# Expert down bias from one stacked pass of score and table rows, scores turned later and copied by the scalar engine

## What is computed

```python
logits = x @ router_weight.T + router_bias
top_val, top_idx = jax.lax.top_k(logits, 4)
router_scores = zeros.at[rows, top_idx].set(softmax(top_val))      # (T, E)
gate_up = einsum('th,ehd->etd', x, gate_up_proj) + gate_up_proj_bias[:, None, :]
glu = gate * sigmoid(gate * 1.702)                                 # gate, up: clipped halves
out = einsum('etd,edh->eth', (up + 1.0) * glu, down_proj) + down_proj_bias[:, None, :]
out = (out * router_scores.T[:, :, None]).sum(axis=0)
```

## Time and profile before

| | us |
|---|---|
| three runs: median (lowest to highest) | 222.13 (221.68 to 222.31) |
| the profiled execution, its own time | 221.69 |
| its span (first to last instruction) | 219.6 |
| busy in the span: PE / PEld / DVE | 212.3 / 176.9 / 159.5 |
| busy in the span: ACT / POOL | 129.7 / 84.2 |

### The profile page before, as it was taken

The page is one execution under the profiler, slowest core; times in us unless marked ns, Lnnn a source line. Parts: engine busy times, 40 slices in busy tenths (PEclk is TensorE's granted clock), DMA queues, the critical chain, the costliest instruction groups (busy, mean ns, idle before and its releaser), DMA issues.

```text
span 219.6 us, 4392 instructions
## 1 busy us (share of the span) xinstructions
PE 212.3 (97%) x1394; PEld 176.9 (81%) x1394; DVE 159.5 (73%) x438; ACT 129.7 (59%) x248; POOL 84.2 (38%) x70
## 2 busy tenths in 40 slices
PE   7999999998999999999999999999999999999995
PEld 2688766776776789788898898898898898898893
DVE  3579897879468558898895785785786786786754
ACT  2238789859632714656765665675676666666340
POOL 6259989201002010246535615615516516416000
PEclk9999999999999999999999999999999999999999
DMA  6994420000000000031442142142241241310002
GB/s 181 328 383 152 145 100 0 0 4 0 3 0 0 3 0 1 0 87 61 145 143 87 60 143 72 72 143 54 89 143 40 103 143 28 115 48 0 0 0 96
DMA packets 7997, 17.41 MB, mean 79 GB/s; under 512 B 928, under 2 KB 3120, under 8 KB 7856
## 3 DMA queue, kind: packets, MB, share of 16 engines
q1 hardware_dynamic: 7552, 16.94, 23.7%
q10 hardware_dynamic: 432, 0.31, 0.5%
HBM read 16.72 MB, written 0.52 MB: 79 GB/s over the span
## 4 chain that ended last, share of the span: by engine, by line
PE 88%; DVE 5%; ACT 3%; issue 3%; POOL 1%; DVEq 0%; ACTq 0%; POOLq 0%
PE PS L1160 37%; PE PS L1176 20%; PE PS L932 3%; PE PS L1044 3%; PE PS L1029 3%; PE PS L984 3%; PE PS L920 2%; PE PS L1127 2%; ACT pr L438 2%; PE PS L1017 2%; PE PS L946 2%; PE PS L970 2%; PE PS L1205 2%; PE PS L997 2%; PE PS L974 1%
## 5 line engine op out<-in xcount | busy, mean ns | idle before, releaser
L308 POOL TENSOR_TENSOR WLg<-raw_g,WHg 128x1024 fp32r<-128x1024 f32 x16 | 38.3, 2396 | 70.8 <-ACT WHg L408 70.6
L1160 PE MATMUL PS<-XH,WHg 128*128 128x512 f32 x120 | 47.0, 391 | 0.0
L1160 PE MATMUL PS<-XL,WHg 128*128 128x512 f32 x120 | 46.9, 391 | 0.0
L1160 PE MATMUL PS<-XH,WLg 128*128 128x512 f32 x120 | 46.7, 389 | 0.0
L840 DVE TENSOR_SCALAR pt<-pt 128x512 f32<-128x512 f32 x30 | 25.0, 833 | 22.4 <-ACT pt L532 22.4
L1176 PE MATMUL PS<-WHd,HH 128*128 128x256 f32 x120 | 34.0, 283 | 0.0
L1176 PE MATMUL PS<-WLd,HH 128*128 128x256 f32 x120 | 34.0, 283 | 0.0
L1176 PE MATMUL PS<-WHd,HL 128*128 128x256 f32 x120 | 34.0, 283 | 0.0
L532 ACT ACTIVATE pt<-PS,bup 128x512 f32<-128x512 f32 x30 | 20.7, 688 | 15.2 <-PE PS L1160 15.2
L538 ACT ACTIVATE HH<-pt 128x512 fp32r<-128x512 f32 x30 | 18.9, 629 | 16.1 <-DVE pt L844 15.7
L438 ACT ACTIVATE pr<-masked,nmax 128x128 f32<-128x128 f32 x64 | 23.7, 444 | 5.9 <-DVE nmax L718 5.9
(11 more groups left out here) (162 smaller groups left out, 355.8 us busy)
## 6 DMA issues: line engine op xcount, KB each, us to landing
raw_g<-we_d SPq DMA_DIRECT2D x16, 512.0 KB, 4.0
raw_w<-we_d SPq DMA_DIRECT2D x16, 256.0 KB, 2.7
ctxT<-ctxT_d SPq DMA_DIRECT2D x1, 1024.0 KB, 10.4
ctx_sb<-ctx_d SPq DMA_DIRECT2D x1, 1024.0 KB, 12.5
wqkv<-wqkv_d SPq DMA_DIRECT2D x3, 256.0 KB, 4.9
out_d<-x SPq DMA_DIRECT2D x4, 128.0 KB, 1.8
rows<-rows_d SPq DMA_DIRECT2D x1, 264.0 KB, 6.3
x<-x_d ACTq DMA_DIRECT2D x2, 128.0 KB, 3.0
```

The source lines that it names most:

```text
L308: g.tensor_tensor(WLg[slot][:, :, :, :].rearrange("p k g f -> p (k g f)"), raw_g[slot][:, :], WHg[slot][:, :, :, :].rearrange("p k g f -> ...
L1160: i = t.matmul(PS[:, 2 * m + part, :], w[slot][:, k, part, m * P:(m + 1) * P], xx[:, k, :], start=(n == 0), stop=(n == 3 * KD - 1))
```

## The change

The table of biases is written three times into a stack of 80 rows (blocks at rows 0, 32 and 64, zero between). The first two blocks hold its high part, the third its low part. The scores are laid out in the same 80 columns: high, low, high. One float32r product over the 80 rows then gives high x high + low x high + high x low.

- SP fetches the table three times, after POOL has zeroed the stack.
- POOL zeroes `dbias`, `low_rows` and `score3`, and makes `dbias3` from the table with three operations: round to `dbias_high`, multiply by `low_rows` (0 in the first 64 rows, -1 in the last 16), add to the table. These stand behind the first `rstds`.
- DVE adds three operations after the score: copy rounded to the high block, subtract for the low block, copy of the high block.
- PE transposes 80 columns instead of 16, after the gate part of the second half of gate_up(1) and no longer between the halves, into bank 6. `weighted_biases` works on `dbias3`.
- The copy to `scoreT` moves from DVE to ACT, behind the two `high` operations of expert 0.

```diff
+            sp.wait_ge(dbias_zero, 1)
+            for block in range(3):
+                sp.dma_start(dbias[block * 32:block * 32 + E, :], dbias_d).then_inc(dbias_in, 16)
...
+            g.memset(dbias[:, :], 0.0).then_inc(dbias_zero, 1)
+            link(g.memset(low_rows[:, :], -1.0))
+            link(g.memset(low_rows[0:64, :], 0.0))
+            g.memset(score3[:, :, :], 0.0).then_inc(score3_zero, 1)
...
-            for n in range(1, 5):
-                rstds(n)
+            rstds(1)
+            pool.wait_ge(dbias_in, 48)
+            g.tensor_copy(dbias_high[:, :], dbias[:, :]).then_inc(dbias_split, 1)
+            pool.wait_ge(dbias_split, 1)
+            g.tensor_scalar(dbias_high[:, :], dbias_high[:, :].bitcast(F32), low_rows[:, 0:1], None, ALU.mult).then_inc(dbias_split, 1)
+            pool.wait_ge(dbias_split, 2)
+            g.tensor_tensor(dbias3[:, :], dbias[:, :], dbias_high[:, :].bitcast(F32), ALU.add).then_inc(dbias_split, 1)
+            rstds(2)
...
                 high(1)
+                if isinstance(e, int) and e == 0:
+                    act.wait_ge(scoreT_ps, 1)
+                    a.activation(scoreT[:, :], PS[0:ROWS3, 6, :], ACT.Copy).then_inc(scoreT_done, 1)
...
-            v_.tensor_tensor(score[:, :, :], esel[:, :, :], erec[:, :].unsqueeze(2).to_broadcast([P, NC, E]), ALU.mult
-                             ).then_inc(score_done, 1)
+            link(v_.tensor_tensor(score[:, :, :], esel[:, :, :], erec[:, :].unsqueeze(2).to_broadcast([P, NC, E]), ALU.mult))
+            dve.wait_ge(score3_zero, 1)
+            high, low_, again = (score3[:, :, n * 32:n * 32 + E] for n in range(3))
+            link(v_.tensor_copy(high.bitcast(F32R), score[:, :, :]))
+            v_.tensor_tensor(low_, score[:, :, :], high, ALU.subtract)
+            v_.tensor_copy(again, high).then_inc(score_done, 1)
...
                 if isinstance(e, int) and e == 0:
-                    dve.wait_ge(scoreT_ps, 1)
-                    v_.tensor_copy(scoreT[:, :], PS[0:E, 5, :]).then_inc(scoreT_done, 1)
                     low(1)
...
-                    i = t.transpose(PS[0:E, 5, c * P:(c + 1) * P], score[:, c, :], ident[:, :])
+                    i = t.transpose(PS[0:ROWS3, 6, c * P:(c + 1) * P], score3[:, c, :], ident[:, :])
...
-                    if m == 0 and isinstance(e, int) and e == 1:
-                        turn_scores()
+                        if m == 1 and part == 0 and isinstance(e, int) and e == 1:
+                            turn_scores()
...
-                pe.wait_ge(dbias_in, 16)
+                pe.wait_ge(dbias_split, 3)
-                    t.matmul(PS[:, 6 + c // 2, (c % 2) * D:(c % 2 + 1) * D], scoreT[:, c * P:(c + 1) * P], dbias[:, :], start=True, stop=True
+                    t.matmul(PS[:, 6 + c // 2, (c % 2) * D:(c % 2 + 1) * D], scoreT[:, c * P:(c + 1) * P], dbias3[:, :], start=True, stop=True
```

More of the change, by code:

```diff
@@ L37 @@
 DW = D * KD
+ROWS3 = 2 * 32 + E
 def decoder_layer(nc, x_d, ctx_d, ctxT_d, wqkv_d, wo_d, params_d, rows_d, mask_d, dbias_d, we_d, out_d):
@@ L69, in decoder_layer @@
         mask8 = sb("mask8", [P, B * M], U8)
-        dbias = sb("dbias", [E, D])
+        dbias = sb("dbias", [ROWS3, D])
+        dbias_high = sb("dbias_high", [ROWS3, D], F32R)
+        dbias3 = sb("dbias3", [ROWS3, D], F32R)
+        low_rows = sb("low_rows", [ROWS3, 1])
         raw_g = [sb(f"raw_g{i}", [P, GU]) for i in range(2)]
@@ L138, in decoder_layer @@
         score = sb("score", [P, NC, E])
-        scoreT = sb("scoreT", [E, T])
+        score3 = sb("score3", [P, NC, ROWS3])
+        scoreT = sb("scoreT", [ROWS3, T], F32R)
         XH = sb("XH", [P, KD, T], F32R)
@@ L200, in decoder_layer @@
         out_done = sem("out_done")
+        dbias_zero, dbias_split, score3_zero, score_parts = (sem(n) for n in ("dbias_zero", "dbias_split", "score3_zero", "score_parts"))
         XS_BANK, XT_BANK, XV_BANK = (7, 2, 4, 5), (3, 4, 6, 3), (1, 2, 4, 5)
@@ L246, in _ @@
             sp.dma_start(ctx_sb[:, :, :], ctx_d.rearrange("b (c p) d -> p (b c) d", p=P)).then_inc(ctx_in, 16)
-            sp.dma_start(dbias[:, :], dbias_d).then_inc(dbias_in, 16)
+            sp.wait_ge(dbias_zero, 1)
+            for block in range(3):
+                sp.dma_start(dbias[block * 32:block * 32 + E, :], dbias_d).then_inc(dbias_in, 16)
             with sp.Fori(1, E // 2) as pair:
@@ L373, in _ @@
             split_keys(1)
-            for n in range(1, 5):
-                rstds(n)
+            rstds(1)
[6 more added lines that the diff above has]
+            rstds(2)
+            rstds(3)
+            rstds(4)
             def expert(e, slot, pair):
```

## The result

| | us |
|---|---|
| changed kernel, four runs: median (lowest to highest) | 220.53 (220.38 to 220.86) |
| kernel before beside it, four runs | 221.91 (221.60 to 222.31) |
| ratio (95% interval) | 0.9941 (0.9926 to 0.9956) |
| profiled execution: its time, its span | 220.86, 219.1 |

The change makes the kernel 0.6% faster, 1.3 us.

What follows compares the result with a forecast made beforehand. TensorE was taken to bound the kernel, with 88% of the last chain. Its possible 1.6 us was limited by two waiting chains to 0.77, and 222.13 less 0.77 gave 221.35 us, range 220.8 to 222.1.

Steps and rivals of the forecast that it cites:

- the sum: Whole kernel: a saving of 0.77 us taken from the profiled 221.69 and from the median 222.13, giving 221.35 us.
- the two chains: Bias to expert 2: waits for scoreT (0.69 to 0.80 us saved) and for expert 2's weights (at most 0.74).
- chain B: Gate/up of expert 2: GpSimd's low weights, 1.16 us later through ScalarE, let PE come at most 0.74 us earlier.
- VectorE's added operations: Behind the score: three small operations delay expert 0's first product by 0.65 us, bounds 0.55 and 0.85.
- ScalarE's scoreT copy: Behind expert 0's two roundings: pitch 0.51 us, so expert 2's high weights (WHg) start 1.16 us later.
- The wait for a signal: From another engine's end to PE's weight load, for scoreT and expert 2's low weights: 0.14 us.
- seen after 0.07: Expert 2's weights: if GpSimd's end is seen after 0.07 us, PE can come 0.81 us earlier.
- What else was taken at nothing: GpSimd's fills, three SyncE transfers, the GpSimd table split and 80-column transposes: hidden behind idle time or waits, zero cost.
- The rival in which that split holds up the low tokens: GpSimd's table split blocks VectorE's low tokens until 55.1; PE 1.4 us later, net +0.6, 222.75 us; chance 0.05.
- the late clamp: VectorE in expert 1: clamp held until GpSimd's weight subtraction ends, about 95.6; the sum would stay the same.
- The chain of expert 1: VectorE's inputs to expert 1's down product: ready by 100.4, 0.6 us to spare; rival losing the gain there, chance 0.06.
- the full 1.6 us: PE around the bias: saving if nothing waited, 220.5 us; part of the more-than-forecast rival (221.15), chance 0.10.

Runs made afterwards that it cites:

- scores rounded by ScalarE: Changed kernel with the score's two high blocks rounded by ScalarE and VectorE's subtraction moved behind expert 0's first product; ratio to before 0.9939.
- moves alone: Kernel before with the later score transposes and the scoreT copy on ScalarE, still 16 rows in plain float32; ratio 0.999.
- pass alone: Kernel before with the bias product as one float32r pass over 16 rows of rounded scores and table, low parts left out; ratio 0.9944.
- changed, four matmuls more: Changed kernel with four tiny 128x8 matmuls on TensorE behind the first fourteen that keep it busy; ratio to before 0.9953.
- copy ahead of the second rounding: Changed kernel with ScalarE's scoreT copy placed before `high(1)` of expert 0; ratio to before 0.9921, median 220.16 us.
- copy given back to VectorE: Changed kernel with the scoreT copy on VectorE again, between its two `low` operations; ratio to before 0.9964, median 221.05 us.
- three fills on the kernel before: Kernel before with three one-column fills added on VectorE ahead of its first statistics; ratio 0.9988.
- scores by ScalarE, three fills: Changed kernel with score high blocks rounded by ScalarE, plus three one-column VectorE fills; run twice, ratios to before 0.9937 and 0.9938.
- the table side: Changed kernel with product, transposes, score and copy put back, leaving fills, three transfers and GpSimd's table split; ratio to before 0.9995.

## Why the prediction was wrong, point by point

**The step that failed.** It is in the sum: "Profiled execution: 221.69 us with a span of 219.6. Less 0.77: 220.9, span 218.8." This keeps 2.1 us around the span, so it puts what the change does outside it at nothing, without a reason. The spans came out as forecast (218.85 on average in the first four executions, 218.88 in the six later ones), but around them there were 1.72 and 1.73 us and no longer 2.1. That is 0.4 of the miss of 0.82. The base from which the saving was subtracted gives another 0.3, and the saving itself 0.1; both are treated below. That the profiled execution took 220.86, where 220.9 was forecast, is luck: its span was the longest of the four (219.1), and that made up for the shorter time outside.

**The direction, the place and the two chains were right.** PE is free after the last gate/up of expert 1, waits for scoreT, then runs four records at 0.58 (0.59 forecast), and loads the weights of expert 2 at 96.02, just behind GpSimd's end at 95.97. The limit that I called chain B binds last, by about 0.1 us: without it the load would stand 0.12 ahead of the first gate/up matmul, as before (96.44 in the earlier trace rows, and the matmul at 96.56), at 95.91. PE's wait for scoreT was shorter than the 0.6 to 0.8 forecast: 0.55 us, from the end of the last gate/up matmul's slot of 0.23 at 92.03 to 92.58.

**The term of the sum: 0.77 forecast, 0.88 to 0.90 in the trace.** Three sizes were off, all to the same side.
- VectorE's added operations: 0.58 and not 0.65. The two with a single input take 0.20 and 0.19 where I put 0.22, and the last gives way after 0.10.
- ScalarE's scoreT copy: 0.47 from start to next start, and not 0.51. WHg came 1.06 later and not 1.16.
- The wait for a signal: 0.14 forecast, 0.04 to 0.05 measured, both behind ScalarE (92.53 to 92.58) and behind GpSimd (95.97 to 96.02). This was a mistake of reading. In the earlier trace rows the bias load comes 0.14 behind the copy, but that distance was not the signal: the copy ended 0.18 behind the start of the last gate/up matmul and the bias started 0.32 behind it; in the kernel with the scores rounded by ScalarE the copy ended 0.26 behind it and the bias still started at 0.32, and so did it in the kernel with the moves alone, where the copy ended 0.13 behind it. The row bounded the delay from above, and I used it as its value.

The bound "seen after 0.07" in the prediction gave 0.81, near the truth, and was given away in the choice.

**The baseline.** I subtracted from 222.13, the median of three runs. With 11 to 23 runs of the same kernel beside the experiments it is 221.74 to 221.84. Some 0.3 to 0.4 us of the miss is this alone; the profiled 221.69, 0.44 below that median, was a warning that I read and did not follow. The range's lower end stood on the same foot.

**What is left.** The measured gain, 1.31 and 1.26 us, is larger than the 0.9 of the middle. Each execution has its own span, so the gain can be parted without a profile. All numbers are us against the kernel before: the middle from one profile each, the rest means over all executions. The changes of the span are good to about 0.15 with eleven executions, and to 0.2 to 0.35 with five or six.

| kernel | DVE instructions (before: 438) | middle | span | outside | total |
|---|---|---|---|---|---|
| pass alone | 438 | -1.24 | -1.26 | 0.00 | -1.27 |
| scores rounded by ScalarE | 438 | -1.35 | -1.33 | -0.05 | -1.38 |
| changed, measured again | 440 | -0.91 | -0.86 | -0.41 | -1.27 |
| changed, four matmuls more | 440 | -0.88 | -0.68 | -0.40 | -1.08 |
| copy ahead of the second rounding | 440 | -1.23 | -1.20 | -0.41 | -1.61 |
| copy given back to VectorE | 441 | -0.82 | -0.33 | -0.38 | -0.70 |
| three fills on the kernel before | 441 | -0.01 | +0.14 | -0.39 | -0.25 |
| scores by ScalarE, three fills | 441 | -1.35 | -0.96, -1.00 | -0.42, -0.38 | -1.38, -1.38 |

So the changed kernel's gain is placed: 0.9 in the stretch that the prediction was about, and 0.4 outside the span, which goes with the longer program of VectorE. The fills show the latter alone, and the kernel that takes two of the three added operations off VectorE again and moves the third loses it. In the changed kernel and the one with the copy ahead, the rest of the span stayed as it was and the total got both. In the three kernels with 441 instructions the span is longer than the middle accounts for: by 0.5 with the copy on VectorE, clear of the scatter; by 0.35 to 0.4 with the scores on ScalarE and the fills, barely clear of it and seen twice; and by 0.15 with the fills alone, no more than the scatter. That the copy on VectorE has a ratio (0.80 us) so near its middle (0.82) is therefore chance: 0.4 were won outside and 0.5 lost within. Why VectorE's program moves the time outside, and what lengthens these spans, stays open.

**What else was taken at nothing** cost nothing: the table side (1.000), the transposes with 80 columns (0.60 as with 16), the split on GpSimd (53.07 to 55.30, forecast until 55.1). The fills on GpSimd are four and not three (`low_rows` is filled twice), and in the changed kernel's trace they too lie ahead of its residual sum. The rival in which that split holds up the low tokens did not come: they take 0.69 as in the earlier trace rows, though GpSimd was scaling and then subtracting beside them:

```profile
54.15 0.69 DVE L729 TENSOR_TENSOR XL<-PS,XH 128x512 fp32r<-128x512 f32 x1 [0.25 <-ACT XH L483]
```

This agrees with the Trainium skill ("SBUF — State Buffer", "SBUF: two separate sides"), by which an operation with one input in PSUM doesn't take the shared port. The prediction's use of the same page for the late clamp held as well: under GpSimd's subtraction, which ran until 95.97, it took 1.07 in place of 0.42 and ended at 96.25, 0.28 behind it. Before it had ended just as far, at 95.93, behind the low down weights, which ran until 95.65. The chain of expert 1 still ended at 100.46, in time for the down product at 101.76. Here the clamp of the changed kernel, and GpSimd's subtraction before:

```profile
95.18 1.07 DVE L867 TENSOR_SCALAR pt<-pt 128x512 f32<-128x512 f32 x1 [0.64 <-ACT pt L552]
```

```profile
94.36 1.29 POOL L315 TENSOR_TENSOR WLd<-raw_w,WHd 128x512 fp32r<-128x512 f32 x1
```

**A rival with the wrong price.** The prediction says that the full 1.6 us would need the scoreT copy ahead of `high(1)`. The kernel with that order gave 1.23 in the middle: once scoreT is early, the low hidden values of expert 0 are late, which the prediction had compared only with a weight load at 92.8.

## What to carry to other kernels

A small matrix product on plain float32 can be worth a stack of high and low rows: eight records became four of half the pitch, and an engine that bounds the kernel got back 1.24 us where nothing was added elsewhere. The stack also keeps the low parts, but its preparation must lie on engines with time to spare. Once a piece of the bounding engine is shortened, list every input that the following pieces need with its ready time; here two of them left 0.9 of a possible 1.6, and moving one copy ahead of one rounding gave 0.35 of it back. Take the delay of a signal only from a row where the receiver had plainly been idle, and for a gain near the noise take more than three runs as the base. Compare the spans of all executions, and not only the total and one profile: it shows whether a gain lies in the work or around it.

## What was not expected of the hardware

- Three one-column fills in VectorE's program, 0.12 us of work in an idle stretch, shortened the time outside the span from 2.09 to 1.71 us. It went with one or two more packets on queue 14, in eight profiles of eight that had more than six packets there (1.69 to 1.77 us), against 2.05 to 2.11 in the six with six packets. The total fell by 0.27 us by its ratio in one kernel and not at all in another, whose span was longer instead, so this is no tool, but it warns against reading the span alone.
- The last gate/up matmul is followed after 0.32 us by the bias where its load was not prepared (91.34 to 91.66 in the earlier trace rows, and the same in the kernel with the pass alone), and after 0.23 where scoreT was there in time (91.60 to 91.83, copy ahead of the second rounding).
